# A delta-rule attention between two FFNs: kept sign of the state, q e^G on GpSimd, softplus summed from PSUM, LZ's first values in one call, and a new order of the pass

## The chip, the cores and the metric

The kernel runs on one core of a Trainium2 chip. The metric is the device time of one execution in microseconds; lower is better. The engines are TensorE (PE; its weight loads are PEld), VectorE (DVE), ScalarE (ACT), GpSimd (POOL) and SyncE (SP), each with its own instruction stream. They meet only at semaphores.

## What is computed

The input x is 8 sequences of 256 tokens with 256 channels. The output is x plus half an FFN, then plus an attention, then plus half an FFN again; all is float32. The FFN phases are not touched. The attention has 16 heads with key and value size 128 and four keys and values (R = 4) per token. Projections pass a causal convolution of four taps and SiLU. Then, for chunks (cut from the reference):

```python
kexp = kg * jnp.exp(Gg)[:, :, :, None, :]
rhs = (vg - jnp.einsum('bhtid,bhdv->bhtiv', kexp, S)).reshape(b, h, C * Rr, dv)
u = jax.scipy.linalg.solve_triangular(M, rhs, lower=True, unit_diagonal=True)
qhat = qg * jnp.exp(Gg)
o = SCALE * (jnp.einsum('bhtd,bhdv->bhtv', qhat, S) + o_intra)
S_new = jnp.exp(glast)[..., None] * S + jnp.einsum('bhtid,bhtiv->bhdv', kdec, u)
```

G is the running sum of log_alpha = -exp(A_log) * softplus(g_raw + dt_bias). At the end o is normalised, gated and projected by Wo.

## The kernel before

Three phases follow each other: FFN, attention, FFN. In the attention the tokens are cut into 4 blocks of 512 (NT), each of two sequences, and each block is worked through head by head: 64 units s = 16 n + h. Chunks are of 8 tokens in 4 groups (32 tokens, 128 rows of keys), so a unit has 16 chunks u = 8 hb + c: two sequences (hb = 0, 1), of 8 steps (c = 0 to 7) each, which the state S ties together.

One loop over p (a **pass**) is written out in each engine's function, as a list of calls in an order found beforehand and fixed by hand; nothing is decided at run time. In a pass, four units are at work at different stages: projection, convolution and decay for p, products and factors for p - 1, inverse for p - 2, the last steps and the output for p - 3. The lists of all engines start with steps 3 to 7 of unit p - 3, and end with steps 0 to 2 of unit p - 2.

The names that matter:
- project_k(b) (b = 4 is q), project_v(b), decay, gate: TensorE products of 512 columns into bank 0 or 1 of PSUM. bank_use lays out in turn which of the two a product takes and which semaphore frees it. tap_k/tap_v (ScalarE) copies the bank times the last tap into acc, conv_k/conv_v (VectorE) add three more taps out of the bank, silu_k/silu_v (ScalarE) write KQ and V.
- decay on ScalarE (Abs, Exp, Ln), above (Relu) and softplus on VectorE give sp_t; add_up sums it into C; distance(l) takes differences of C into rn, factors(l) are their exponentials Fl, Fe and F0; levels(q, l) on VectorE gives X = KQ times Fl for quarter q.
- products(q, l) on TensorE multiplies X with itself into banks 2 and 3. evacuate(q, l) on VectorE copies bank 2 masked into Pd, keep(q) on ScalarE bank 3 into E and At. products(q + 1, 0) waits for both.
- take, norm, weigh (VectorE) build LA from Pd. begin and rows (GpSimd) clear LZ, set its first values and eliminate row by row; unfold and turn (VectorE) bring the result into Zc and Ztc; place, first to fourth (TensorE and ScalarE) make the inverse Ztf of it.
- spread(q, what) on GpSimd is kdec (what 0) and kexp (1): KQ times e^(G end - G) or e^G (Fe). turn on TensorE transposes kdec. query (VectorE) makes qn, the product of q and -e^G.
- One step: rhs (TensorE, kexp times S; VectorE makes Rs), solve (TensorE; ScalarE copies to Us), update (TensorE: kdT times Us, At times Us, S times qn; VectorE makes the new S). In between stands S with alternating sign from step to step, by the SUB at its end; qn's sign and rhs's ADD fit that.
- out_square (ScalarE) squares the output, mean_square (TensorE) sums it, out_root and gated normalise, output multiplies by WO.

The same engine serves all four units in turn, so a late operand holds up everything behind it on that engine. ScalarE needs another function table for SiLU and Tanh than for Exp and Ln; preload_act_table_set and the compiler place the loads (ACT_TABLE_LOAD).

Of the kernel before, what the change touches and what calls it, by code (L numbers as in the profile page):

```python
# [88 lines left out]
def build(nc, x, out, wkq, wv, wo, vec, wf1, wg1, wb, bg1, wu, wd, fvec, wsd, cst, B, H):  # L89
# [4 lines left out]
    with ctx:  # L94
# [22 lines left out]
        half_c = [cs[:, C_SEL + 16 + half:C_SEL + 17 + half] for half in range(2)]  # L117
# [453 lines left out]
        LZ = sb("LZ", [P, 32, 16])  # L571
# [31 lines left out]
        v_max, v_kq, v_d, v_qn, v_X, v_Pd, v_bd = (sem(f"v_{n}") for n in ("max", "kq", "d", "qn", "X", "Pd", "bd"))  # L603
# [4 lines left out]
        g_zero, g_kdec, g_kexp, g_copy, g_X0, g_init, g_row = (sem(f"g_{n}") for n in ("zero", "kdec", "kexp", "copy", "X0", "init", "row"))  # L608
# [3 lines left out]
        def turns(order, count):  # L612
# [117 lines left out]
        def delta_tensor(e):  # L730
# [176 lines left out]
            def update(s, hb, c):  # L907
# [13 lines left out]
                if c:  # L921
                    ins = mm(o, S[:, hb, c % 2, :], qn[:, s % 2, 32 * u:32 * u + 32], False, True)
# [1012 lines left out]
```

## Time and profile before

| | |
|---|---|
| median of 3 runs | 5054.45 us |
| lowest to highest | 5050.53 to 5068.83 us |
| the profiled execution | 5059.32 us |
| its span, first to last instruction | 5057.5 us |
| TensorE, VectorE, ScalarE, GpSimd busy | 90, 82, 69, 64% of the span |
| mean granted clock of TensorE | 0.967 |

The profile is one execution, taken with the hardware profiler. Busy time is the union of an engine's instructions; idle time is put down to the semaphore event that ended it. The span's first 330 us are the first FFN and the ramp of the attention, its last 260 us the second FFN; between them passes of the loop repeat. The granted clock is the share of TensorE's full 2.4 GHz that was let through.

### The profile page before, as it was taken

The numbers are of one execution on the slowest core, as the hardware profiler recorded it, in microseconds if no ns is written. First come the engines' busy times: TensorE is split into PE (matmuls) and PEld (weight loads), VectorE is DVE, ScalarE is ACT, GpSimd is POOL, SyncE is SP. The second block draws the span as 40 slices with busy tenths as digits, with TensorE's granted clock in tenths as the row PEclk, the third lists the DMA queues.
The fourth block names the chain that finished last, engine by engine and source line by source line (L and its number), as shares of the span: only waits on it lengthen the run. The fifth ranks groups of instructions, "written<-read, shape, count | busy, mean of one in ns | idle before, by whom it ended". The sixth has DMA issues, their size and how long they took to land.

```text
span 5057.5 us, 151421 instructions
## 1 busy us (share of the span) xinstructions
PE 4558.3 (90%) x63200; PEld 3167.2 (63%) x63200; DVE 4143.8 (82%) x7262; ACT 3476.3 (69%) x6771; POOL 3221.5 (64%) x5316
## 2 busy tenths in 40 slices
PE   8869999999999999999999999899999999998889
PEld 5436666666666666666666666666666666666655
DVE  3278998888888889889999889988899888998422
ACT  3267777777777777777777777777777777777421
POOL 0047777776677766777767777667777777767500
PEclk9989999999999999999999999999999999999769
DMA  2110000000100000000100000000000000000010
GB/s 89 65 48 20 25 25 25 25 13 25 33 31 21 21 25 25 25 14 24 33 31 29 24 14 25 25 25 20 22 29 25 25 25 14 25 25 9 3 45 18
DMA packets 49724, 135.45 MB, mean 27 GB/s; under 512 B 7056, under 2 KB 28176, under 8 KB 48400
## 3 DMA queue, kind: packets, MB, share of 16 engines
q1 hardware_dynamic: 49040, 125.77, 7.2%
q8 instruction: 498, 8.16, 0.7%
q14 instruction: 186, 1.52, 0.1%
HBM read 111.60 MB, written 14.16 MB: 25 GB/s over the span
## 4 chain that ended last, share of the span: by engine, by line
PE 55%; DVE 26%; ACT 11%; issue 6%; POOL 1%; DMA 1%; SPq 0%; DVEq 0%; ACTq 0%
PE bank L734 46%; DVE acc L1392 8%; PE bank L256 7%; DVE X L1389 7%; DVE sp_t L1389 2%; ACT L1299 2%; DVE Pd L1497 2%; ACT Us L1048 1%; ACT o L1049 1%; DVE Zc L1576 1%; DVE o L1392 1%; DVE Rs L1392 1%; PE bank L805 1%; ACT L1329 1%; DVE x1m L1389 1%
## 5 line engine op out<-in xcount | busy, mean ns | idle before, releaser
L1392 DVE SCALAR_TENSOR_TENSOR acc<-bank,vc,acc 128x510 f32<-128x510 f32 (+2 forms) x1728 | 1271.4, 739 | 144.6 <-ACT acc L1048 118.9
L1813 POOL TENSOR_TENSOR LZ<-LZ,LT 128x120 f32<-128x120 f32 (+26 forms) x1984 | 961.6, 485 | 155.5
L1810 POOL TENSOR_TENSOR LT<-LA,LZ 128x120 f32<-128x120 f32 (+26 forms) x1984 | 913.4, 460 | 145.8
L1389 DVE TENSOR_TENSOR X<-KQ,Fl 128x640 f32<-128x640 f32 x1024 | 1004.3, 997 | 1.5 <-ACT Fl L1049 1.5
L1783 POOL COPY X<-KQ 128x640 f32<-128x640 f32 x256 | 246.8, 964 | 928.6 <-PE bank L734 311.8
L734 PE MATMUL bank<-X 128*32 128x60 f32 (+1 forms) x32768 | 656.2, 206 | 134.6 <-DVE Pd L1497 87.2
L734 PEld LDWEIGHTS bank<-X 128*32 128x32 f32 x32768 | 529.3, 112 | 370.3 <-issue 210.7
L1048 ACT ACTIVATE Us<-bank 128x128 f32<-128x128 f32 x1024 | 280.8, 276 | 628.5 <-PE bank L734 622.5
L734 PE MATMUL bank<-xnTm,WK 128*128 128x512 f32 x1280 | 663.3, 644 | 47.2 <-DVE acc L1392 33.8
L734 PE MATMUL bank<-Rs,Ztf 128*128 128x128 f32 x2048 | 475.6, 319 | 67.9 <-DVE Rs L1392 47.5
L1762 POOL TENSOR_TENSOR kdec<-KQ,Fe 128x512 f32<-128x512 f32 x256 | 339.0, 1324 | 297.9 <-PE bank L805 297.9
L1392 DVE SCALAR_TENSOR_TENSOR Rs<-V,knT,bank 128x128 f32<-128x128 f32 x896 | 308.4, 344 | 257.9 <-PE bank L734 246.3
L734 PE MATMUL bank<-xnTm,WV 128*128 128x512 f32 x1024 | 498.4, 609 | 12.8 <-ACT sg L1049 7.4
L734 PE MATMUL bank<-Us,kdT 128*128 128x128 f32 x1792 | 412.3, 313 | 71.5 <-ACT Us L1048 56.7
L734 PEld LDWEIGHTS bank<-Rs,Ztf 128*128 128x128 f32 x2048 | 322.0, 194 | 195.6 <-DVE Rs L1392 116.1
L1048 ACT ACTIVATE acc<-bank,vc 128x512 f32<-128x512 f32 x576 | 394.0, 684 | 66.7 <-PE bank L734 63.3
L734 PEld LDWEIGHTS bank<-xnTm,WK 128*128 128x128 f32 x1280 | 232.1, 201 | 284.0 <-issue 190.3
L734 PE MATMUL bank<-S,kexp 128*128 128x128 f32 x1792 | 393.3, 302 | 5.0 <-ACT S L1048 3.4
L1762 POOL TENSOR_TENSOR kexp<-KQ,Fe 128x512 f32<-128x512 f32 x256 | 388.6, 1528 | 0.0
L734 PEld LDWEIGHTS bank<-Us,kdT 128*128 128x128 f32 x1792 | 275.6, 194 | 137.6 <-ACT Us L1048 125.8
L734 PE MATMUL bank<-qn,S 128*128 128x32 f32 x1792 | 353.9, 280 | 0.0
L734 PEld LDWEIGHTS bank<-S,kexp 128*128 128x128 f32 x1792 | 286.7, 195 | 79.0 <-issue 32.8
(145 smaller groups left out, 9370.0 us busy)
## 6 DMA issues: line engine op xcount, KB each, us to landing
WK<-in_wkq SPq DMA_DIRECT2D x64, 704.0 KB, 6.1
WV<-in_wv SPq DMA_DIRECT2D x64, 576.0 KB, 3.9
WO<-in_wo SPq DMA_DIRECT2D x64, 128.0 KB, 2.0
wuh<-in_wu SPq DMA_DIRECT2D x2, 1024.0 KB, 7.6
xt<-in_x SPq DMA_DIRECT2D x4, 512.0 KB, 6.5
wuh_d<-wuh SPq DMA_DIRECT2D x1, 2048.0 KB, 6.3
x_d<-x SPq DMA_DIRECT2D x4, 512.0 KB, 3.1
xnT_d<-xT SPq DMA_DIRECT2D x4, 512.0 KB, 2.7
```

Source lines behind the costliest of these rows:

```text
L256: return e.matmul(o, l, r, start=start, stop=stop, skip_group_check=True)
L734: return e.matmul(o, l, r, start=start, stop=stop, skip_group_check=True)
L805: ins = e.transpose(o[:, P * c:P * c + P], kdec[:, c, :], ident)
L1048: return e.activation(o, i, f, scale=scale)
L1299: e.preload_act_table_set("natural_log_exp_and_others")
L1389: return e.tensor_tensor(o, a, b, op)
L1392: return e.scalar_tensor_tensor(out=o, in0=a, scalar=sc, in1=b, op0=op0, op1=op1)
L1497: return e.copy_predicated(o, mk, d.rearrange("p n (a c) -> p n a c", c=c))
L1762: return e.tensor_tensor(o.rearrange("p u (g i t) -> p (u g) i t", g=4, i=R), kq[:, 16 * q:16 * q + 16, 0:R, :], f.unsqueeze(2).broadcast_ ...
L1783: e.tensor_copy(X0[:, :, 0:40], kk.rearrange("p g i t -> p g (i t)")).then_inc(g_copy, 1)
L1810: e.tensor_tensor(tmp, LA[:, j + 1:32, 8 * (j % R) + j // R].unsqueeze(2).broadcast_to([P, rr, cc]), LZ[:, j, 0:cc].unsqueeze(1).broadcast ...
L1813: e.tensor_tensor(LZ[:, j + 1:32, 0:cc], LZ[:, j + 1:32, 0:cc], tmp, SUB).then_inc(g_row, 1)
```

## The change

- *The state keeps its sign.* S is written by adding, Rs by subtracting, and the copy at step 0 has no factor -1.
- *q e^G on GpSimd.* query leaves VectorE's list and stands in GpSimd's as one tensor_tensor, with semaphore g_qn instead of v_qn. The wait for it moves from a unit's first update to the matmul that reads qn.
- *Softplus.* above writes the Relu back into the PSUM bank, softplus adds the bank and rn.
- *LZ's first values.* After the memset one tensor_tensor over 8 x 2 x 2 elements, in place of four tensor_scalar over 8; LZ's tile gets 16 elements longer for the view.
- *Order.* The lists of calls of all four engines and the turns of the two banks and three acc are laid out anew. One preload before factors(3) and one before decay(2) are gone.

```diff
-        half_c = [cs[:, C_SEL + 16 + half:C_SEL + 17 + half] for half in range(2)]
+        half_c = cs[:, C_SEL + 16:C_SEL + 18]
...
-        LZ = sb("LZ", [P, 32, 16])
+        LZt = sb("LZ", [P, 8 * 66])
+        LZ = LZt[:, 0:512].rearrange("p (r c) -> p r c", c=16)
+        LZd = LZt[:, :].rearrange("p (t x) -> p t x", x=66)[:, :, 0:64].rearrange("p t (h y) -> p t h y", y=32)[:, :, :, 0:18:17]
...
-            ("decay", 0, 0, a_relu, 1, 0), ("v", 1, 1, v_cv, 12, 5), ("k", 3, 0, v_ck, 15, 11),
+            ("decay", 0, 0, v_sp, 1, 0), ("k", 3, 0, v_ck, 15, 11), ("ms", 0, 3, a_ms, 3, 0),
...
-                    w.wait_ge(v_qn, every(s, 1))
...
                 if c:
+                    w.wait_ge(g_qn, every(s, 1))
                     ins = mm(o, S[:, hb, c % 2, :], qn[:, s % 2, 32 * u:32 * u + 32], False, True)
...
-                act(sp_t[:, :], bank[bank_use["decay", 0, s][0]][:, :], ACT.Relu, bias=dtb[:, h:h + 1]).then_inc(a_relu, 1)
+                raw = bank[bank_use["decay", 0, s][0]][:, :]
+                act(raw, raw, ACT.Relu, bias=dtb[:, h:h + 1]).then_inc(a_relu, 1)
...
-                act(S[:, hb, 1, :], bank[5 + hb][:, 2 * P:3 * P], ACT.Copy, scale=-1.0).then_inc(a_S, 1)
+                act(S[:, hb, 1, :], bank[5 + hb][:, 2 * P:3 * P], ACT.Copy).then_inc(a_S, 1)
...
-                tt(sp_t[:, :], sp_t[:, :], rn[:, 0, :], ADD).then_inc(v_sp, 1)
+                w.wait_ge(a_F, every(s - 1, 12))
+                tt(sp_t[:, :], bank[bank_use["decay", 0, s][0]][:, :], rn[:, 0, :], ADD).then_inc(v_sp, 1)
...
-                stt(Rs[:, hb, :], V[:, s % 2, u, :], knT[:, s % 2, u:u + 1], bank[5 + hb][:, 0:P], MUL, ADD).then_inc(v_Rs, 1)
+                stt(Rs[:, hb, :], V[:, s % 2, u, :], knT[:, s % 2, u:u + 1], bank[5 + hb][:, 0:P], MUL, SUB).then_inc(v_Rs, 1)
...
-                    MUL, SUB).then_inc(v_S, 1)
+                    MUL, ADD).then_inc(v_S, 1)
...
+                w.wait_ge(p_o, every(s - 2, 16))
+                e.tensor_tensor(qn[:, s % 2, :].rearrange("p (g t) -> p g t", t=8), KQ[:, s % 2, :, R, :],
+                                Fe[:, 0, :].rearrange("p (g t) -> p g t", t=8), MUL).then_inc(g_qn, 1)
...
-                        e.tensor_scalar(flat[:, a:a + 463:66], Cn[:, :, 2 * hf + k], half_c[hf], None,
-                                        MUL).then_inc(g_init, 1)
+                e.tensor_tensor(LZd, Cn[:, :, :].rearrange("p t (h k) -> p t h k", h=2),
+                                half_c.unsqueeze(1).unsqueeze(3).broadcast_to([P, 8, 2, 2]), MUL).then_inc(g_init, 1)
```

**TensorE from mean_square to output.** Rows of the program before, then of the changed one (o,cs is mean_square, WK a projection of k or q, X products, WO output, fgm,WV the gate):

```order
L734 MATMUL bank<-o,cs 128x512
L734 MATMUL bank<-xnTm,WK 128x512 x2
L734 MATMUL bank<-X 32x60 x16
L734 MATMUL bank<-X 32x20 x32
L734 MATMUL bank<-X 32x40 x8
L734 MATMUL bank<-X 32x80 x8
L734 MATMUL bank<-WO,o 128x256 x4
L734 MATMUL bank<-fgm,WV 128x512
L796 MATMUL bank<-cs,V 128x128 x4
```

```order
L736 MATMUL bank<-o,cs 128x512
L736 MATMUL bank<-X 32x60 x16
L736 MATMUL bank<-X 32x20 x16
L736 MATMUL bank<-xnTm,WK 128x512 x2
L736 MATMUL bank<-X 32x20 x16
L736 MATMUL bank<-X 32x40 x8
L736 MATMUL bank<-X 32x80 x8
L736 MATMUL bank<-fgm,WV 128x512
L736 MATMUL bank<-WO,o 128x256 x4
L736 MATMUL bank<-xnTm,WV 128x512 x4
```

project_k(4) stood directly behind mean_square and now has products(1,0) and (1,1) ahead of it; the gate went from behind the output to ahead of it; turn_v(0) left this place.

**ScalarE from the last of steps 0 to 2 into the next pass.** Us is the copy of solve, Fl a factor, KQ silu_k, acc a tap, kdT the transposed kdec; before, then now:

```order
L1048 ACTIVATE Us<-bank 128x128 x2
L1299 ACT_TABLE_LOAD
L1049 ACTIVATE Fl<-rn,posA 128x32x8
L1049 ACTIVATE Fl<-rn,negA 128x32x8
L1048 ACTIVATE Us<-bank 128x128
L1048 ACTIVATE kdT<-bank 128x512
L1049 ACT_TABLE_LOAD
L1049 ACTIVATE KQ<-acc 128x64x8 x2
L1048 ACTIVATE acc<-bank,vc 128x512
L1048 ACTIVATE Us<-bank 128x128
L1048 ACTIVATE kdT<-bank 128x512
```

```order
L1051 ACTIVATE Fl<-rn,posA 128x16x16
L1051 ACTIVATE Fl<-rn,negA 128x16x16
L1050 ACTIVATE Us<-bank 128x128 x3
L1051 ACT_TABLE_LOAD
L1051 ACTIVATE KQ<-acc 128x64x8
L1050 ACTIVATE Us<-bank 128x128
L1050 ACTIVATE kdT<-bank 128x512
L1051 ACTIVATE KQ<-acc 128x64x8
L1050 ACTIVATE acc<-bank,vc 128x512
L1050 ACTIVATE Us<-bank 128x128
L1051 ACTIVATE KQ<-acc 128x64x8
L1308 ACT_TABLE_LOAD
```

A load stood between two Us, with factors(3) behind it; now the factors come ahead of the last steps' Us and the three silu_k stand under one load.

**VectorE, the softplus sum and the evacuations of the first two quarters.** sp_t is the sum, X levels, Pd evacuate, knT lengths, acc a convolution, o gated; before (the sum then stood much later in the pass) and now:

```order
L1392 SCALAR_TENSOR_TENSOR acc<-bank,vc,acc 128x2x254
L1392 SCALAR_TENSOR_TENSOR acc<-bank,vc,acc 128x2x253
L1392 SCALAR_TENSOR_TENSOR acc<-bank,vc,acc 128x2x255
L1392 SCALAR_TENSOR_TENSOR acc<-bank,vc,acc 128x2x254
L1497 COPY_PREDICATED Pd<-cs,bank 128x80
L1392 SCALAR_TENSOR_TENSOR acc<-bank,vc,acc 128x2x253
L1497 COPY_PREDICATED Pd<-cs,bank 128x40x2
L1497 COPY_PREDICATED Pd<-cs,bank 128x20x4
L1392 SCALAR_TENSOR_TENSOR qn<-KQ,Fe 128x512
L1392 SCALAR_TENSOR_TENSOR o<-sg,o 128x512
L1392 SCALAR_TENSOR_TENSOR o<-bank,hon,o 128x512
```

```order
L1392 SCALAR_TENSOR_TENSOR Rs<-V,knT,bank 128x128
L1558 STREAM_TRANSPOSE knT<-kn 128x32
L1392 SCALAR_TENSOR_TENSOR Rs<-V,knT,bank 128x128
L1389 TENSOR_TENSOR sp_t<-bank,rn 128x512
L1389 TENSOR_TENSOR X<-KQ,Fl 128x640
L1489 COPY_PREDICATED Pd<-cs,bank 128x80
L1389 TENSOR_TENSOR X<-KQ,Fl 128x640
L1489 COPY_PREDICATED Pd<-cs,bank 128x40x2
L1392 SCALAR_TENSOR_TENSOR acc<-bank,vc,acc 128x2x255
L1489 COPY_PREDICATED Pd<-cs,bank 128x20x4
L1392 SCALAR_TENSOR_TENSOR acc<-bank,vc,acc 128x2x254
L1392 SCALAR_TENSOR_TENSOR acc<-bank,vc,acc 128x2x253
```

The two evacuations that stood behind four convolutions now stand between X and convolutions, qn is gone, and sp_t and knT have come in behind the last two Rs.

## Rows read from the trace of the kernel before

**Rows 1.** The page: busy us of each engine, its share of the span, instructions.

```profile
PE 4558.3 (90%) x63200; PEld 3167.2 (63%) x63200; DVE 4143.8 (82%) x7262; ACT 3476.3 (69%) x6771; POOL 3221.5 (64%) x5316
```

**Rows 2.** LZ's memset; a stretch: its us, each engine's busy us, clock, DMA, GB/s.

```profile
L1792 POOL MEMSET LZ<- x64: 521/525/527, 332.4 to 4745.0; 128x512 f32 x64
...
1400.00:2400.00 1000.00, 915.21 (x13692) 644.05 (x13692) 891.74 (x1552) 741.01 (x1461) 719.79 (x1188) 0.98 0.07 24
```

**Rows 3.** TensorE's waits between 400 and 4600 us: us in total, times, longest.

```profile
PE bank L734 <- DVE Pd L1497: 78.8, 55, 1.5
PE bank L734 <- ACT Us L1048: 54.2, 120, 0.5
PE bank L734 <- ACT o L1049: 46.7, 60, 0.8
PE bank L734 <- issue: 42.4, 78, 2.1
PE bank L734 <- DVE Rs L1392: 39.4, 120, 0.4
PE bank L734 <- DVE acc L1392: 26.2, 60, 0.4
```

**Rows 4.** The chain that ended last, 2500 to 2572 us: start, us, what.

```profile
2533.23 1.28 ACT L1049
...
2540.16 0.57 DVE acc L1392
...
2549.53 1.09 DVE Zc L1576 x2
...
2560.90 1.67 DVE sp_t L1389
2562.79 1.52 issue
```

**Rows 5.** TensorE's timeline: start, us, what, idle time before it and its releaser.

```profile
2502.77 1.96 PE L734 MATMUL bank<-xnTm,WK 128*128 128x512 f32 x4
...
2539.25 1.10 PE L734 MATMUL bank<-o,cs 128*128 128x512 f32 x2 [0.78 <-ACT o L1049]
2540.78 3.56 PE L734 MATMUL bank<-xnTm,WK 128*128 128x512 f32 x4 [0.43 <-DVE acc L1392]
...
2564.59 0.63 PE L734 MATMUL bank<-X 128*32 128x60 f32 x32 [1.44 <-DVE Pd L1497]
```

**Rows 6.** Stretches of 2 us behind mean_square, in two passes; columns as in Rows 2.

```profile
2540.96:2542.96 2.00, 2.00 (x3) 0.79 (x4) 1.34 (x4) 1.90 (x5) 1.76 (x4) 0.52 0.00 0
2542.96:2544.96 2.00, 2.00 (x57) 0.69 (x57) 0.95 (x2) 0.58 (x1) 1.61 (x6) 0.63 0.00 0
...
2682.96:2684.96 2.00, 1.71 (x100) 1.07 (x99) 1.59 (x3) 1.44 (x4) 1.75 (x4) 1.00 0.00 0
```

**Rows 7.** Timelines of VectorE and GpSimd in the later half of a pass.

```profile
2560.81 1.76 DVE L1389 TENSOR_TENSOR sp_t<-sp_t,rn 128x512 f32<-128x512 f32 x1
...
2565.18 0.78 DVE L1389 TENSOR_TENSOR X<-KQ,Fl 128x640 f32<-128x640 f32 x1
...
2566.89 1.27 POOL L1762 TENSOR_TENSOR kdec<-KQ,Fe 128x512 f32<-128x512 f32 x1 [3.19 <-PE bank L805]
```

**Rows 8.** Groups of instructions: count, busy us, mean ns; then one row of GpSimd's timeline.

```profile
L1389 DVE TENSOR_TENSOR x1m<-bank,x1m 128x512 f32<-128x512 f32 x128 | 88.6, 692 | 15.5 <-PE bank L734 15.4
...
L1392 DVE SCALAR_TENSOR_TENSOR qn<-KQ,Fe 128x512 f32<-128x512 f32 x64 | 43.8, 684 | 0.0
...
L1798 POOL TENSOR_SCALAR LZ<-Cn,cs 128x8 f32<-128x8 f32 x256 | 123.7, 505 | 6.4
...
2545.51 0.22 POOL L1810 TENSOR_TENSOR LT<-LA,LZ 128x16 f32<-128x16 f32 x1
```

**Rows 9.** ScalarE's timeline around the load ahead of factors(3).

```profile
2513.93 1.28 ACT L1299 ACT_TABLE_LOAD   x1
...
2516.04 0.26 ACT L1048 ACTIVATE Us<-bank 128x128 f32<-128x128 f32 x1
```

More of the change, by code:

```diff
@@ L606, in build @@
         v_Rs, v_S, v_o, v_out = (sem(f"v_{n}") for n in ("Rs", "S", "o", "out"))
-        g_zero, g_kdec, g_kexp, g_copy, g_X0, g_init, g_row = (sem(f"g_{n}") for n in ("zero", "kdec", "kexp", "copy", "X0", "init", "row"))
+        g_zero, g_kdec, g_kexp, g_qn, g_copy, g_X0, g_init, g_row = (sem(f"g_{n}") for n in ("zero", "kdec", "kexp", "qn", "copy", "X0", "init", "row"))
         def turns(order, count):
@@ L964, in delta_tensor @@
                 solve(p - 3, 0, 5)
-                products(p - 1, 0, 3)
                 rhs(p - 3, 1, 5)
@@ L968, in delta_tensor @@
                 solve(p - 3, 1, 5)
+                products(p - 1, 0, 2)
+                rhs(p - 3, 0, 6)
+                products(p - 1, 0, 3)
+                update(p - 3, 1, 5)
                 decay(p)
-                rhs(p - 3, 0, 6)
-                update(p - 3, 1, 5)
+                rhs(p - 3, 1, 6)
+                solve(p - 3, 0, 6)
                 products(p - 1, 0, 4)
-                solve(p - 3, 0, 6)
-                rhs(p - 3, 1, 6)
                 solve(p - 3, 1, 6)
@@ L1030, in delta_tensor @@
                 update(p - 2, 1, 0)
+                project_k(p + 1, 2)
+                rhs(p - 2, 1, 1)
                 update(p - 2, 0, 1)
-                rhs(p - 2, 1, 1)
-                turn(p - 1, 2)
+                solve(p - 2, 1, 1)
                 rhs(p - 2, 0, 2)
-                solve(p - 2, 1, 1)
                 update(p - 2, 1, 1)
                 solve(p - 2, 0, 2)
+                products(p, 0, 0)
                 rhs(p - 2, 1, 2)
                 update(p - 2, 0, 2)
-                products(p, 0, 0)
                 solve(p - 2, 1, 2)
+                rhs(p - 2, 0, 3)
+                update(p - 2, 1, 2)
         def delta_scalar(e):
@@ L1677, in delta_vector @@
                 rhs(p - 3, 0, 7)
[L1678 to L1689 removed]
+                lengths(p - 2)
+                rhs(p - 3, 1, 7)
+                softplus(p)
+                levels(p - 1, 1, 2)
+                evacuate(p - 1, 0, 1)
+                levels(p - 1, 1, 3)
+                evacuate(p - 1, 0, 2)
+                conv_k(p, 3, 2)
+                evacuate(p - 1, 0, 3)
+                conv_k(p, 3, 1)
+                conv_k(p, 3, 0)
+                levels(p - 1, 1, 4)
                 gated(p - 3, 0)
+                levels(p - 1, 2, 1)
                 gated(p - 3, 1)
@@ L1713, in delta_vector @@
                 conv_v(p - 1, 3, 0)
+                levels(p - 1, 3, 1)
+                levels(p - 1, 3, 2)
                 evacuate(p - 1, 2, 0)
                 evacuate(p - 1, 2, 1)
-                evacuate(p - 1, 2, 2)
-                levels(p - 1, 3, 1)
-                softplus(p)
-                levels(p - 1, 3, 2)
-                evacuate(p - 1, 2, 3)
-                clamp(p)
-                lengths(p - 2)
                 levels(p - 1, 3, 3)
                 add_up(p)
+                clamp(p)
                 levels(p - 1, 3, 4)
+                evacuate(p - 1, 2, 2)
                 distance(p, 1)
+                evacuate(p - 1, 2, 3)
+                conv_k(p + 1, 0, 2)
+                conv_k(p + 1, 0, 1)
                 evacuate(p - 1, 3, 0)
+                conv_k(p + 1, 0, 0)
                 evacuate(p - 1, 3, 1)
+                scale(p)
                 evacuate(p - 1, 3, 2)
```

275 lines of the change are left out of this document (124 added, 151 removed).

## The prediction, made before the changed kernel ran

> **What bounds the kernel now.** I read the page first, then where time is evenly spent, then the waits, then the chain. The page [rows 1] has TensorE busy 90% of the span, VectorE 82%, ScalarE 69%, GpSimd 64%. The middle phase is nearly all of it: GpSimd clears LZ once per head and block, 64 times between 332.4 and 4745.0 us [rows 2], so a pass of the loop takes (4745.0 - 332.4) / 63 = 70.0 us. A stretch of 1000 us [rows 2] says that in it TensorE is busy 91.5%, VectorE 89% and GpSimd 72%, at a mean granted clock of 0.98; the one behind it reads the same within 1%. TensorE idles about 6 us of each pass. That, and what the clock loses, is all that can be won: no matrix product is removed. The waits of TensorE between 400 and 4600 us, which are 60 passes [rows 3], divide it, per pass: 78.8 / 60 = 1.31 us for Pd (products(3,0) needs the last evacuate of quarter 2), 54.2 / 60 = 0.90 for Us, 46.7 / 60 = 0.78 for the squared output ahead of mean_square, 42.4 / 60 = 0.71 for issue, 39.4 / 60 = 0.66 for Rs, 26.2 / 60 = 0.44 for acc (project_k(4), whose bank is still read by the convolution).
>
> The chain of one pass [rows 4] shows why Pd is late. From 2549.5 to 2562.6 it runs on VectorE alone: the unfolding into Zc, four X, six acc, X and the softplus sum sp_t. VectorE is thus the limit of the later half of a pass, although its busy share is the lower one. Earlier in the pass the chain goes over a table load on ScalarE and three convolutions to project_k(4), 0.43 us late [rows 4, 5]. From there I call the start of mean_square, 2539.25 [rows 5], M.
>
> **The clock.** The four matmuls of project_k(4) take 3.56 us in this pass, those of another projection 1.98 [rows 5]. The granted clock is 0.52 in the 2 us from 2540.96, that is the 1.2 GHz level, and 1.00 at the same place two passes later [rows 6]; of ten passes looked at, three fell. TensorE had idled 0.78 and 0.43 us ahead of the fall. By the mean of 0.98 the clock costs 0.02 x 70 = 1.4 us a pass. One fall costs (1 - 0.52) x 2 + (1 - 0.63) x 2 = 1.7 us [rows 6].
>
> **The change, part by part.** *The sign of the state* changes the scale of a copy and the second operator of three VectorE forms, and no count or shape: 0.
>
> *The softplus sum.* It took 1.76 us as sum of two SBUF tensors while GpSimd ran kdec and kexp; an equal sum with one operand in PSUM (x1m) has a mean of 0.69 [rows 7, 8]. VectorE gets 1.76 - 0.69 = 1.07 us back. The Relu now writes into the bank, so that the bank is freed by the sum instead of by the Relu: its next user is mean_square. Laying the rows end to end, the sum ends some 3 us ahead of M. Cost 0; if decay were 3 us late, every further us would stand ahead of mean_square.
>
> *The product q e^G* leaves VectorE, 0.68 us [rows 8], and costs GpSimd about what kdec costs there, 1.27 us [rows 7]. GpSimd is idle 28% of the time [rows 2], 19.6 us a pass, so there it is free. It is put between kdec of quarter 2 and kexp of quarter 3. Its first reader on TensorE comes most of a pass later. What it does delay, by its own 1.3 us, is kexp of quarter 3, for which the next head's Fe on ScalarE waits: the rows put that kexp's end at M + 29.7 and Fe at M + 31.4. 0 on the path, and 1.3 if that cover were gone.
>
> *LZ's first values.* Four calls of 0.505 us [rows 8] become one with 32 elements. No row has that form; a product of 16 elements takes 0.22 [rows 8], and four of the old calls 2.0: between these I take 0.4, as it is one instruction on few elements. GpSimd's elimination, from the clearing of LZ to the unfolding, gets 1.6 us shorter, and another 1.3 since kdec of quarter 3 no longer stands in it. The unfolding, which now stands earlier on VectorE (about M + 7 rather than M + 10), then still finds it finished, by about 1 us.
>
> *Table loads.* ScalarE had seven per pass and has four, by the order of both; each takes 1.28 us, so 3.85 us of its time go. Off the bound, but one of them stood between two Us [rows 9]: the Us copy at 2516.04 came late, and update(0,3) waited for it 0.54 us.
>
> *The new order* decides the rest. I added the durations of the rows from M on, each engine in its new order.
> - Us. update(0,1) now has project_k(2) ahead of it, and update(0,3) has no table load ahead of its Us: both waits (0.90) go. But update(1,0) comes 0.3 us behind solve(0,1), and update(0,5) directly behind rhs(1,5); I put 0.4 for these. Net -0.5.
> - project_k(4) has the first two products of quarter 1 ahead of it, 1.0 us of TensorE work, and the convolutions of k3 end in that time: -0.44.
> - The bank of output(0) was mean_square's and is now project_k(4)'s. It is free when the convolutions of k4 are done. ScalarE copies k4 only behind both roots, a table load and silu_v(0): M + 4.3 to 5.0. Three convolutions of 0.74 end at M + 7.3. TensorE is there at M + 6.3: a new wait of **+1.0**. Bounds 0.2 (as the edge of this kind now costs) and 2.0 (VectorE late by one more operation).
> - Pd. VectorE has the softplus sum and one X fewer ahead of the unfolding's successors, but three X, the running sum, clamp and distance(1) are pulled ahead of the last evacuate of quarter 2; TensorE has project_k(0) and half of the second inverse pulled ahead of products(3,0). The rows put the evacuate's end at M + 26.3 and TensorE at M + 26.4: the wait of 1.31 shrinks to 0.1, **-1.2**. The bounds are -1.31 and +0.5, since the adding-up has no collisions beyond two.
> - Rs and S between steps 3 and 7: a pass now has 2 us less other work between its steps. I put **+0.2**; bounds 0 and 1.0.
> - mean_square still stands right behind the last update: 0.78 stays. Issue stays.
> - Clock. The 0.43 us behind the 0.78 goes, but 1.0 us of idling comes 6 us later. I take **-0.4** of 1.4; bounds -1.4 and +0.7.
>
> Sum per pass: -0.5 - 0.44 + 1.0 - 1.2 + 0.2 - 0.4 = -1.34 us. The prologue, the epilogue and both FFN phases are untouched. Over 63 passes -84 us. The profiled execution took 5059.3 us with a span of 5057.5, the median of the runs is 5054.45; 5059.3 - 84 = 4975, and against the median **4970 us**.
>
> **Two rules of the skill.** The collision of VectorE and GpSimd is in the rows: an X takes 0.78 us alone, and the sum of two SBUF tensors takes 1.76 while GpSimd multiplies [rows 7]. The Trainium skill (GPSIMD Engine Reference, Specifications) states that GpSimd's SBUF interfaces are shared with VectorE, with contention for VectorE instructions with two SBUF inputs. It speaks against moving q e^G: a ninth product per pass is on the shared interface. By it the moved product can take up to its own 1.27 us back from VectorE instead of giving 0.68.
> The sum out of PSUM is measured at 0.69 us [rows 8]. The Trainium skill (VectorE: DVE Perf Modes, the section on the TRN2 errata) gives PSUM sources a larger fixed part than SBUF sources, 120 cycles to 58, by which, as an estimate, 0.06 us of the gain would be lost; the trace's row is used.
>
> **Rivals.** *A: more collisions.* Slower. Four operations of VectorE are doubled in a pass now, about 1.0 us each (two X, sp_t, rn). In the new order GpSimd's kexp of quarters 1 and 2 and kdec of quarter 1 come at about M + 16 to M + 21, over levels(3,1) to levels(3,3); kdec of quarter 2, q e^G and kexp of quarter 3 over scale and distance(1), kdec of quarter 3 over distance(2). If six are hit instead of four, VectorE gets 2.0 us more, in the half of the pass where it is the limit, and TensorE pays all of it: -1.34 + 2.0 = +0.66, 5054 + 42 = 5096. It decides as soon as the collisions outgrow the slack, which after the sum above is about zero. For it: nine products instead of eight and a nearly full VectorE. Against: the unavoidable waits of GpSimd for kdec's bank spread them, and softplus is out of it.
> The skill's rule above is this rival's mechanism; the trace agrees on the collisions of today and cannot show the new ones.
> *B: the clock.* The idle of 1.0 us ahead of output(0) joins the 0.78 and the clock falls in every pass: 1.7 a pass and other losses of 0.4, so 2.1 instead of 1.4. The sum is -1.34 + 0.4 + 0.7 = -0.24, 5039. For it: three of ten passes fall behind 1.2 us of idling spread over 2.5. Against: here 3.8 us of dense work lie between.
> *C: VectorE is clear of the path.* Convolutions of k4 end as TensorE arrives (-0.8), and the clock hardly falls (-0.8 more): -2.9 a pass, 4870. For it: 1.75 us of VectorE work and 3.85 of ScalarE's are gone for certain.
> *D: nothing arrives.* The order trades waits one for one; it gives about B's time and is counted there.
>
> **Chances.** Forecast 0.52 (4920 to 5020), A 0.16, B and D 0.18, C 0.14. About 0.5%, 25 us, is what a measurement of this kernel can tell from no change. Faster by more: 0.52 + 0.14 + 0.02 of B = 0.68; within: 0.16; slower: 0.16. The range reaches into C and A, 4890 to 5075, and leaves about 0.2 out.
>
> **What would show it.** The clearings of LZ should come 68.7 us apart. TensorE's waits: Us below 30 us, Pd below 20 in 60 passes, acc at output(0) up to 60, o unchanged near 47. VectorE: sp_t at 0.69 a piece, about 1.7 us less busy per pass. ScalarE: 4 x 64 table loads, not 7 x 64. GpSimd: qn near 1.3 us. Wrong would be: X and rn with a larger mean (A); a mean clock at or below 0.97 (B); the unfolding waiting for LZ, or more than 2 us of waits for Rs, then steps 3 to 7 have become a latency chain, for which I allowed 0.2.

## The result, and the profile after

The changed kernel takes **5279.07 us** (median of 4 runs, 5271.58 to 5306.96), against 5052.49 us for the kernel before on the same chip. The ratio is **1.0461**, with a 95% interval of 1.0431 to 1.0491. The forecast was 4970 us in a range up to 5075: wrong in sign, and 204 us above the upper end.

The page of the changed kernel, as [rows 1]: busy us of each engine; below it the DMA queues (packets, MB, share of 16 engines).

```profile
PE 4729.6 (90%) x63200; PEld 3382.8 (64%) x63200; DVE 3918.7 (74%) x7198; ACT 3197.8 (61%) x6572; POOL 3048.7 (58%) x5188
...
q1 hardware_dynamic: 49040, 125.77, 6.8%
q8 instruction: 498, 8.16, 0.6%
```

LZ's memset and the stretch of [rows 2], of the changed kernel:

```profile
L1792 POOL MEMSET LZ<- x64: 524/524/528, 337.6 to 4990.6; 128x512 f32 x64
...
1400.00:2400.00 1000.00, 905.46 (x13194) 657.85 (x13192) 798.38 (x1449) 651.12 (x1355) 636.34 (x1075) 0.92 0.07 24
```

A pass takes (4990.6 - 337.6) / 63 = 73.86 us against 70.04 [rows 2]: +3.8. VectorE, ScalarE and GpSimd all have less to do. TensorE is as busy as before, but at a granted clock of 0.92 instead of 0.98, so that it gets less done: 13194 matmuls in the stretch, against 13692.

Its waits between 400 and 4600 us, as [rows 3], here 57 passes:

```profile
PE bank L736 <- issue: 150.6, 63, 4.4
PE bank L736 <- DVE acc L1392: 108.7, 114, 1.9
PE bank L736 <- DVE Rs L1392: 46.5, 166, 0.5
PE bank L736 <- ACT o L1051: 44.4, 57, 0.8
PE bank L736 <- ACT Ztf L1050: 13.2, 56, 0.2
```

The waits for Pd and Us are gone. Those for semaphores went about as planned. The first row did not: **issue**, idle time that no semaphore ends, was 42.4 us over 60 passes [rows 3] and is 150.6 over 57. From here on I call a piece of it, over 0.15 us long, a **stand**.

One such stand, on TensorE's timeline (start, us, what, idle time before it), in a pass whose mean_square starts at 2581.82 (M):

```profile
2581.82 1.10 PE L736 MATMUL bank<-o,cs 128*128 128x512 f32 x2 [0.78 <-ACT o L1051]
...
2589.58 1.75 PE L736 MATMUL bank<-WO,o 128*128 128x256 f32 x7 [1.64 <-DVE acc L1392]
...
2591.47 3.71 PE L736 MATMUL bank<-xnTm,WV 128*128 128x512 f32 x8
2595.41 0.69 PE L736 MATMUL bank<-Zc,E 32*32 32x32 f32 x32 [0.24 <-ACT Ztf L1050]
2596.03 1.50 PE L736 MATMUL bank<-X 128*32 128x60 f32 x112
...
2597.52 0.19 PE L736 MATMUL bank<-Ys,Ztf 32*32 32x32 f32 x1
2600.31 0.22 PE L736 MATMUL bank<-Ztf,Ys 32*32 32x32 f32 x2 [2.60 <-issue]
```

TensorE stops in the middle of second(0), between two matmuls that have no wait between them in the program. Ahead of the stop run project_v(3), first(0) and products(2,0) to products(2,3) without a break. From first(0) to products(2,4) there are 208 short matmuls, each with its weight load: 416 instructions. (The trace has every float32 matmul as two.) I call them **the run**. Stretches of 2 us of the same pass (columns as in Rows 2: us, busy us of PE, PEld, DVE, ACT, POOL, clock, DMA share, GB/s):

```profile
2594.00:2596.00 2.00, 1.76 (x35) 0.77 (x33) 2.00 (x4) 1.31 (x2) 0.00 (x0) 1.00 0.00 0
2596.00:2598.00 2.00, 1.71 (x123) 1.51 (x115) 1.97 (x4) 1.07 (x2) 1.24 (x2) 1.00 0.89 279
2598.00:2600.00 2.00, 0.00 (x0) 0.00 (x0) 1.93 (x4) 0.00 (x0) 2.00 (x3) 1.00 1.05 230
2600.00:2602.00 2.00, 1.69 (x61) 1.63 (x61) 2.00 (x2) 0.83 (x3) 0.64 (x1) 0.69 0.94 385
2602.00:2604.00 2.00, 2.00 (x17) 1.45 (x13) 1.68 (x5) 0.91 (x3) 0.00 (x0) 0.50 0.42 172
...
2614.00:2616.00 2.00, 2.00 (x6) 0.80 (x6) 2.00 (x4) 1.11 (x3) 0.00 (x0) 0.90 0.00 0
```

Three things coincide: 123 matmuls in 2 us, the DMA engines full from 2596 to 2602 (SyncE's load_wv and load_wk, 576 and 704 KB, issued when project_v(3) is done), and TensorE at a stand. Behind it the clock goes to 0.50, the 1.2 GHz level, until 2614.4. Over passes 3 to 59, a 128x512 matmul takes 1103 ns at that level and 611 at the full clock, one of 128x128 429 and 298, and the shortest 237 and 192.

What is late is the program itself. The queue q8 moved 498 packets of 8.16 MB / 498 = 16.4 KB. TensorE's records are 127,591 (63,200 matmuls, as many weight loads, 1,191 of its sequencer), 256 to a packet: q8 carries TensorE's instructions, some 7.5 packets a pass. The DMA queues from M + 3.2 to M + 15.8, and in the 1.6 us behind that:

```profile
q1 hardware_dynamic: 232, 0.54, 14.6%
...
q1 hardware_dynamic: 180, 0.44, 116.8%
q8 instruction: 1, 0.02, 4.2%
```

In the first stretch there is no packet of q8, and the next one comes when q1 already fills the engines. That packet takes from 2597.74 to 2598.81; TensorE had stopped at 2597.71 and goes on at 2600.31, 1.5 us after the landing.

The records settle that this is no coincidence. I numbered TensorE's records in the order of their start. Modulo 256, all 69 stands of passes 3 to 59 of the changed kernel come at the number 193 or 194, and all 453 stands of 1 us or more in the 14 kernels below at 193 to 195. Behind each of these 453, TensorE goes on 1.2 to 1.65 us after the packet for the next block has landed. Such a stand is thus a wait for the next packet, in the kernel before too. (Some 40 of the stands there, of 0.3 us at M + 4, come at any number and are of another kind.)

The Trainium skill (Runtime: NRT & Kernel Launch, Instruction fetch mechanics) has instructions fetched in blocks of 256 while earlier ones run, at a cost "mostly hidden". The blocks agree with the 498 packets and with the places of the stands; the cost is not hidden here, 2.88 us a pass.

**All passes.** I counted passes 3 to 59 of every kernel (a pass is from one mean_square to the next; a fall is a spell of the 1.2 GHz level; the last four columns are us per pass).

| kernel | ratio to before | us a pass | stands | other waits | us at 1.2 GHz |
|---|---|---|---|---|---|
| before | 1 | 70.14 | 0.70 | 4.65 | 2.2 |
| after | 1.0461 | 74.25 | 2.88 | 3.78 | 12.3 |
| e1_late_loads | 0.9834 | 68.56 | 1.28 | 3.78 | 2.9 |
| e2_before_late_loads | 1.0001 | 70.12 | 0.63 | 4.73 | 2.2 |
| e3_late_wk | 1.0204 | 72.17 | 2.12 | 3.76 | 9.2 |
| e4_edits_old_order | 0.9992 | 70.22 | 0.75 | 4.64 | 2.5 |
| e5_late_spread | 0.9867 | 68.95 | 1.03 | 3.83 | 3.7 |
| e6_spread | 1.0318 | 72.65 | 2.63 | 3.86 | 8.7 |
| e7_double_loads | 1.0516 | 74.44 | 3.24 | 3.76 | 11.9 |
| e8_before_loads_on_run | 1.0182 | 71.55 | 1.37 | 4.70 | 3.7 |
| e9_after_loads_on_second_run | 1.0112 | 71.13 | 2.19 | 3.70 | 6.8 |
| e10_late_v_inside | 0.9835 | 69.16 | 0.45 | 5.47 | 2.2 |
| e11_late_products_ahead | 0.9602 | 67.17 | 0.45 | 4.15 | 0.4 |
| e12_products_ahead | 0.9626 | 67.21 | 0.49 | 4.15 | 0.2 |

Passes with neither fall nor stands over 0.3 us take 68.80 us before (14 of 57) and **65.79** after (7 of 57). The plan itself was good, by 3.0 us a pass. Seven passes are few, but the undisturbed passes of e1 (13) and e7 (4) take 65.86 and 65.83. The mean of all passes of the changed kernel is 8.5 us above 65.79: 2.9 are the stands, and the other 5.6, which I put down to the 12.3 us at half clock, are the remainder.

### The profile page after: what moved, and what is told of

Read it like the earlier page. It is cut to its first block, busy times and chain, and to the rows that moved or that the text cites. A ratio compares the mean times of both kernels' runs of the same rounds, so it can differ in the third digit from the quotient of the medians.

```text
span 5281.2 us, 150966 instructions
## 1 busy us (share of the span) xinstructions
PE 4729.6 (90%) x63200; PEld 3382.8 (64%) x63200; DVE 3918.7 (74%) x7198; ACT 3197.8 (61%) x6572; POOL 3048.7 (58%) x5188
## 3 DMA queue, kind: packets, MB, share of 16 engines
q8 instruction: 498, 8.16, 0.6%
## 4 chain that ended last, share of the span: by engine, by line
PE 65%; DVE 15%; ACT 10%; issue 9%; POOL 1%; DMA 0%; DVEq 0%; SPq 0%; ACTq 0%; POOLq 0%
PE bank L736 52%; PE bank L256 7%; DVE acc L1392 4%; PE bank L798 4%; ACT Ztf L1050 2%; PE bank L807 2%; DVE LA L1523 2%; ACT acc L1050 2%; ACT o L1051 2%; ACT L1051 2%; DVE Zc L1568 1%; DVE Rs L1392 1%; DVE X L1389 1%; DVE rn L1389 1%; DVE Ztc L1576 1%
## 5 line engine op out<-in xcount | busy, mean ns | idle before, releaser
L1809 POOL TENSOR_TENSOR LZ<-LZ,LT 128x120 f32<-128x120 f32 (+26 forms) x1984 | 931.4, 469 | 155.5
L1389 DVE TENSOR_TENSOR X<-KQ,Fl 128x640 f32<-128x640 f32 x1024 | 944.6, 932 | 0.0
L736 PE MATMUL bank<-xnTm,WK 128*128 128x512 f32 x1280 | 695.9, 671 | 24.9 <-DMA WK<-in_wkq 12.2
L736 PE MATMUL bank<-X 128*32 128x60 f32 (+1 forms) x32768 | 614.3, 206 | 77.0 <-issue 66.5
L1783 POOL COPY X<-KQ 128x640 f32<-128x640 f32 x256 | 184.9, 722 | 645.3 <-PE bank L736 348.3
L736 PEld LDWEIGHTS bank<-xnTm,WK 128*128 128x128 f32 x1280 | 253.7, 214 | 276.2 <-issue 252.0
L736 PE MATMUL bank<-Us,kdT 128*128 128x128 f32 x1792 | 387.7, 299 | 20.5 <-ACT Us L1050 0.2
L736 PE MATMUL bank<-S,kexp 128*128 128x128 f32 x1792 | 376.3, 298 | 0.6 <-ACT S L1050 0.2
L1439 DVE TENSOR_SCALAR rn<-bank 128x512 f32<-128x512 f32 x64 | 44.2, 691 | 411.3 <-PE bank L736 411.3
L736 PEld LDWEIGHTS bank<-Zc,E 32*32 32x32 f32 (+1 forms) x6144 | 256.3, 137 | 144.2 <-ACT Ztf L1050 89.4
```

Of the source, the lines that this page charges most:

```text
L736: return e.matmul(o, l, r, start=start, stop=stop, skip_group_check=True)
L1389: return e.tensor_tensor(o, a, b, op)
L1783: e.tensor_copy(X0[:, :, 0:40], kk.rearrange("p g i t -> p g (i t)")).then_inc(g_copy, 1)
L1809: e.tensor_tensor(LZ[:, j + 1:32, 0:cc], LZ[:, j + 1:32, 0:cc], tmp, SUB).then_inc(g_row, 1)
```

## The experiments

The theories by letter: **S**, bulk loads that fall on a run of short matmuls keep TensorE's instruction packets waiting. **R**, the run asks for instructions faster than they can come, loads or none. **W**, the longer wait at output(0) lowers the clock, and that is the root. Where an edit is "late loads", it is this line ahead of SyncE's loads of a pass:

```
+                if 0 <= p - 2 < NS:
+                    w.wait_ge(p_rhs, nth(p - 2, 14, 1))
                 s = p - 1
                 if 0 <= s < NS:
...
                         load_wv(s + 2)
```

It holds them until rhs(1,1). In e1 they move mostly from M + 39 to M + 45, where TensorE starts some 20 to 30 matmuls in 2 us, against 141 in the densest 2 us of the run. Nothing else differs.

### Loads late, in the changed kernel, in the kernel before, and in part; and the edits without the order

*e1_late_loads*: the changed kernel with late loads.

> The changed kernel; SyncE issues the loads of WV and WK (and of the block's inputs) only when rhs(1,1) of unit p - 2 is done, some 38 us behind mean_square instead of 14. Nothing else changes. Theory S (supply): in the changed kernel TensorE stands 2 to 4 us inside the second inverse or products of quarter 2, where it waits for no semaphore, because its next instructions are fetched by DMA behind 1.28 MB of weight loads; that idle time then drops the clock. Expected: the stalls under 'issue' fall from 150 us to under 50, mean granted clock of the middle phase 0.98 or more, passes 66 to 67 us apart, 4800 to 4860 us. Rival R (run): the run of short matmuls outpaces the fetch, whatever the loads do: stalls stay, 5230 to 5290 us. Rival W (wait): the clock falls because of the 1.64 us wait for acc ahead of the output: it stays too, clock near 0.92, over 5200 us.

Measured: 4978.96 us, ratio **0.9834** [0.9797, 0.987]. One line takes 300 us away, and the kernel beats both. But it misses what was expected by 120 us. Its waits:

```profile
PE bank L738 <- DVE acc L1394: 116.5, 122, 1.9
PE bank L738 <- issue: 75.4, 62, 1.9
```

The wait for acc at output(0) is as long as in the changed kernel (1.64 us a piece), while the passes with a fall are down from 42 to 14: W is out. Stands of 1.1 to 1.9 us are left inside the run in 31 of 57 passes, with no load in sight. So S holds for most of it, and R for a part.

*e2_before_late_loads*: the kernel before with the same line.

> The kernel before, with the same delay of the loads. Theory S: it too loses something to the fetch, but has less short work in one run; its waits under 'issue' are 42 us in 60 passes and its clock 0.98. At most these go: 5057 - 40 - 50 = 4960, at least 5040. Rivals R and W: no change, 5045 to 5060.

Measured: 5055.04 us, ratio 1.0001 [0.9985, 1.0016]. That is in the range of R and W; S had expected 5040 at most. In the old order the loads cost nothing that can be measured: stands are 0.63 us a pass instead of 0.70.

*e3_late_wk*: the line stands only ahead of load_wk, 704 of 1280 KB.

> The changed kernel, with the load of WK alone delayed (0.70 of the 1.28 MB); WV stays where it is. Theory S: the burst ends some 2 us behind its start instead of 4, so the fetch is late by 2 us less: about half or more of the loss goes, 4850 to 5080 us. Rivals R and W: 5230 to 5290 us.

Measured: 5163.51 us, ratio 1.0204 [1.0168, 1.024], outside what was expected: 116 us of the 300 that late loads win, where half or more had been expected. 576 KB in the same place are enough for stands of 2 us and more in 30 of 57 passes.

*e4_edits_old_order*: the order of before, with the sign, q e^G on GpSimd, and LZ's values in one call; the softplus sum stays in SBUF, and the preloads stay.

> The kernel before, its order of calls kept, with the sign of the state, q e^G on GpSimd (between kexp of quarter 2 and kexp of quarter 3) and LZ's first values in one call; the softplus sum stays in SBUF. My theory of the parts: VectorE gets 0.68 us a pass back ahead of gated, where it waits for ScalarE, GpSimd 1.6 us: 0 to -0.5 us a pass, 5020 to 5055 us. A rival in which one of these edits is itself the cost of the change (more collisions on GpSimd) expects over 5080.

Measured: 5049.73 us, ratio 0.9992 [0.9967, 1.0016]. That is within what was expected. These edits alone are worth nothing that can be measured. What the change gives and takes is in the order, with the softplus sum and the two preloads that go with it.

### Run spread out, loads doubled

*e5_late_spread* and *e6_spread* change TensorE's list at one place; e5 has the late loads as well.

```
                 products(p - 1, 2, 1)
+                second(p - 2, 0)
                 products(p - 1, 2, 2)
+                turn_v(p - 2, 0)
                 products(p - 1, 2, 3)
-                second(p - 2, 0)
-                products(p - 1, 2, 4)
-                turn_v(p - 2, 0)
                 third(p - 2, 0)
                 turn_v(p - 2, 1)
+                products(p - 1, 2, 4)
```

> The changed kernel with the late loads of the first run, and TensorE's order of one stretch spread: second(0) stands after products(2,1), turn_v(0) after products(2,2), third(0) after products(2,3), and products(2,4) last, so that longer matmuls of the turns and third lie between the groups of short ones. Theory R (the run first(0), products(2,0..3), second(0), products(2,4) asks for instructions faster than they arrive, whatever the loads do): the idle time of TensorE that nothing ends by a semaphore falls from 1.28 us a pass (late loads alone) to under 0.6, and falls of the clock with it; period 67.2 to 68.0 against 68.56, so 4895 to 4945 us. Rival (the rest of the stalls is another cause, or second(0) now waits for GpSimd's or VectorE's part of first): stalls stay at 1.2 us or semaphore waits at second(0) appear, 4970 to 5030 us.

Measured: 4984.77 us, ratio 0.9867 [0.9842, 0.9892]. Stands 1.03 instead of 1.28 us, 22 passes with a fall instead of 14: a miss, in the rival's range. In first(0), products(2,0), products(2,1), second(0) and products(2,2) there are still 176 matmuls together, with their weight loads 352 instructions, more than a packet has.

> The changed kernel with TensorE's order spread in the same way, and the loads where the change has them. Theory S (SyncE's bulk loads hold back the instruction packets of TensorE's queue): the packet is late by as much as before, but it is wanted later or earlier only by the phase of the pass, so stalls fall from 2.9 us a pass to 1.5 to 2.5 and the time from 5279 to 5100 to 5220 us. Theory R (the density of the run alone): stalls under 1 us a pass and 4900 to 5000 us. If neither bears: 5250 to 5300 us.

Measured: 5208.94 us, ratio 1.0318 [1.0284, 1.0351]. The time is within the range of S. Its 1.5 to 2.5 us of stands were 2.63.

*e7_double_loads*: SyncE copies about as many bytes from memory to memory once more, ahead of load_wv.

```
+                        w.wait_ge(p_gate, every(s, 1))
+                        w.wait_ge(p_v, every(s, 4))
+                        w.wait_ge(d_spare, 32 * s)
...
+                        e.dma_start(spare_d[0, :, 0:nk], ws).then_inc(d_spare, 16)
+                        e.dma_start(spare_d[1, :, 0:nv], vs).then_inc(d_spare, 16)
                         load_wv(s + 2)
```

> The changed kernel with copies from memory to memory of about the bytes of one pass's WK and WV issued just ahead of the loads, at the same place of the pass; no engine waits for them but SyncE. Theory S: the instruction packet lies behind twice the burst, stalls grow from 2.9 us a pass to 4.5 to 7, the half clock with them, and the time is 5380 to 5650 us. Theory R: stalls as in the changed kernel, 5270 to 5320 us.

Measured: 5311.95 us, ratio 1.0516 [1.0479, 1.0554]. The time is in the range of R, not of S: stands 3.24 us, not 4.5 to 7, and the interval overlaps that of the changed kernel. The loads now move from M + 14 to M + 22 instead of M + 14 to M + 18. The mere form of S, that a packet waits until the burst is over, falls: twice the bytes cost 0.36 us more of stands. R alone falls by e1, whose run is the same. I therefore took each packet's delay from the records: a packet begins when TensorE has come to a certain instruction, so the time since it passed the earliest such place among the neighbouring packets says how late it is. Of the packets due at M + 14 to M + 16, the mean is 1.8 us with late loads (72 packets), 4.0 in the changed kernel (73), 4.7 with the doubled ones (72). (With more or fewer neighbours each mean moves by up to 0.4.) So a burst costs a packet some 2 to 3 us, whether it is long or very long. The delay is an inference from start times; no row shows the request for a packet.

### Loads moved onto another run

Both hold the loads until total(p), so that they move at M + 23 to M + 28 in e8 and mostly at M + 25 to M + 29 in e9, onto the second run of short matmuls.

```
+                if 0 <= p < NS:
+                    w.wait_ge(p_norm, every(p, 1))
                 s = p - 1
```

*e8_before_loads_on_run*, in the kernel before:

> The kernel before, with SyncE holding the loads of WV and WK until total(p), so that they move some M+23 to M+28, on the kernel's own second run of short matmuls (products(3,0), first(1), products(3,1), second(1), products(3,2), products(3,3)). Theory S (bulk loads that fall on a run of short matmuls hold back TensorE's instructions, in any order of the work): idle time of TensorE that nothing ends grows from 0.7 to 1.5 to 2.5 us a pass, part of the passes lose the clock, 5110 to 5280 us. Rival (the loads only hurt the changed order, by something else in it): no change, 5045 to 5065 us.

Measured: 5145.67 us, ratio 1.0182 [1.0142, 1.0222]. That is within the range of S. So the old order can be hurt in the same way; S does not hang on the new one. TensorE's waits:

```profile
PE bank L736 <- DVE Pd L1499: 83.1, 58, 1.5
PE bank L736 <- issue: 82.7, 84, 3.2
```

The wait for Pd stays, issue doubles against [rows 3]. Stands of 1.5 us and more appear behind M + 26 in 24 of 57 passes; in the kernel before there was none. The stands come to 1.37 us a pass, a little under what was expected.

*e9_after_loads_on_second_run*, in the changed kernel:

> The changed kernel with the same hold, until total(p): the loads leave the first run (M+14) and meet the second (second(1), products(3,0) to products(3,4), M+26 to M+28). Theory S: the stalls move with the loads, from M+16 to M+28, 2 to 3 us a pass, falls follow them there, 5120 to 5280 us. Rival (only the place of the first run is at fault, and any later time for the loads is as good as the latest): 4970 to 5000 us as with the loads at M+38.

Measured: 5114.11 us, ratio 1.0112 [1.0075, 1.0148], 6 us under the range. Stands of 2 us and more went from M + 16 to M + 28, in 20 passes; all 20 fell there. The place of the loads decides where the stands are.

### The run cut by a long product

*e10_late_v_inside*: late loads, and project_v(3) between products(2,1) and products(2,2); second(0) also moves, ahead of products(2,3).

> The changed kernel with the loads at M+38, and project_v(3), two long matmuls' pairs of some 1.9 us with few instructions, put between products(2,1) and products(2,2) instead of ahead of the run. Theory R (what stalls are left come from the run's density alone, with packets that take their usual time): stalls at M+14 to M+20 go from 0.8 to under 0.2 us a pass, and with them most falls of the clock (14 of 57 passes with late loads alone); 66.8 to 67.6 us a pass, 4870 to 4920 us. Rival: as with late loads alone, 4970 to 4990 us.

Measured: 4981.62 us, ratio 0.9835 [0.9808, 0.9863]. All stands at M + 14 to M + 24 are gone, 0 of 57 passes, as R says. The time did not follow and lies in the rival's range, for project_v(3) had been the cover of another wait:

```profile
PE bank L738 <- ACT Ztf L1052: 119.0, 61, 2.0
...
PE bank L738 <- issue: 26.2, 27, 1.9
```

first(0) now waits 1.96 us for Ztf in every pass, and the clock falls behind that in 19 of 57, without a stand.

*e11_late_products_ahead* and *e12_products_ahead* put two products ahead of project_v(3) instead, e11 with late loads, e12 with the loads where the change has them.

```
+                products(p - 1, 2, 0)
+                products(p - 1, 2, 1)
                 project_v(p - 1, 3)
                 first(p - 2, 0)
-                products(p - 1, 2, 0)
-                products(p - 1, 2, 1)
                 products(p - 1, 2, 2)
-                products(p - 1, 2, 3)
                 second(p - 2, 0)
+                products(p - 1, 2, 3)
                 products(p - 1, 2, 4)
```

> The changed kernel with the loads at M+38, and TensorE's order changed in one place: products(2,0), products(2,1), project_v(3), first(0), products(2,2), second(0), products(2,3), products(2,4). The 64 short matmuls and loads of products(2,0..1) run ahead of project_v(3), whose 1.9 us cover the wait for Ztf that cost 1.96 us with project_v(3) inside the run. Theory: no stall at M+14 to M+20 as in that run, first(0) waits at most 0.3 us, so a pass takes 66.0 plus 0.4 of stalls at M+28 plus some 0.6 for the clock that is left, 67.0, 4870 to 4910 us. Rival (the clock falls for other reasons in a third of the passes whatever the stalls are, as 19 of 57 did there): 68.0 to 68.6 a pass, 4930 to 4980 us.

Measured: **4854.87 us**, ratio **0.9602** [0.9573, 0.9631], below the range by 15 us. Its interval and that of e12, below, overlap.

> The changed kernel with the same change of TensorE's order, and the loads where the change has them, M+14 to M+18. If bulk loads alone make the stalls: as the changed kernel, 5250 to 5290 us. If the run's density alone: as with the loads late, 4870 to 4980 us. If it takes both, dense run and loads at once: stalls under 1 us a pass, some passes still fall, 4920 to 5060 us.

Measured: 4869.68 us, ratio 0.9626 [0.9601, 0.965]. Taken by itself this is the lower edge of "the run's density alone" in the expectation, and below the range of "both". The four kernels together say more:

| | loads where the change has them | loads late |
|---|---|---|
| the change's order | 5279.07 (after) | 4978.96 (e1) |
| two products ahead of project_v(3) | 4869.68 (e12) | 4854.87 (e11) |

Loads cost 300 us on the long run and 15 on the shortened one, where the intervals overlap; the long run costs 124 us without loads and 409 with them. With 64 short matmuls (128 instructions with their weight loads) fewer behind project_v(3), 144 instead of 208, the loads may stay where they were. The large loss takes both, a dense run and loads at once; some 30% of it comes with the run alone. The waits and the same place of a pass in e12 (stretches from M + 13.4 on):

```profile
PE bank L736 <- DVE acc L1392: 116.4, 122, 1.9
PE bank L736 <- DVE Rs L1392: 52.3, 186, 0.5
PE bank L736 <- ACT o L1051: 49.0, 63, 0.8
PE bank L736 <- DVE Pd L1489: 41.6, 63, 3.0
PE bank L736 <- issue: 28.4, 31, 1.9
```

```profile
2190.00:2192.00 2.00, 2.00 (x28) 0.76 (x28) 1.97 (x4) 0.15 (x1) 2.00 (x3) 1.00 0.00 0
2192.00:2194.00 2.00, 1.90 (x125) 1.71 (x121) 0.96 (x2) 1.49 (x4) 2.00 (x2) 1.00 0.54 118
2194.00:2196.00 2.00, 2.00 (x33) 1.69 (x28) 1.93 (x4) 1.62 (x4) 0.10 (x1) 1.00 1.01 417
```

The DMA engines are as full as in the changed kernel (1.01, 417 GB/s), the matmuls as dense (125 in 2 us), but the density is over when the burst comes. At this place TensorE has no stand over 0.6 us in 57 passes, and the clock stays at 1.00. The new wait for Pd, 0.66 us a pass, is the price of the earlier products.

**Do the stands bring the falls?** For the run at M + 14 (and the one at M + 28 in e8 and e9), by the longest stand in it:

| kernel | stand of 2 us or more: passes, with a fall | shorter or none: passes, with a fall |
|---|---|---|
| after | 42, 42 | 15, 0 |
| e1 | 0, 0 | 57, 11 |
| e3 | 30, 28 | 27, 5 |
| e5 | 1, 1 | 56, 16 |
| e6 | 35, 34 | 22, 6 |
| e7 | 45, 44 | 12, 2 |
| e8 | 15, 15 | 42, 17 |
| e9 | 20, 20 | 37, 2 |
| e10 | 0, 0 | 57, 19 |
| e12 | 0, 0 | 57, 0 |

Of the 17 falls of e8 without a long stand, ten come at M + 26, behind the wait for Pd, as ten do in the kernel before; the 19 of e10 come behind the wait of 1.96 us for Ztf. The 11 of e1 all follow a stand of 1.1 to 1.9 us. Over all kernels, behind M + 13, a fall began during or within 5.5 us behind 3 of 223 stands below 1 us, 41 of 145 from 1 to 1.5, 59 of 104 from 1.5 to 2, and 184 of 188 above. In the same place with the same loads the clock falls when TensorE stood long, and does not when it didn't. That bulk loads lower the clock by themselves is excluded by e12.

## Why the prediction was wrong

**The step that failed is "Issue stays".** The stands rose from 0.7 to 2.9 us a pass, and brought most of 5.6 more through the clock. The rows had the warning: 42.4 us of issue, the longest 2.1 [rows 3], and 1.52 us of it in the chain [rows 4]. I took idle time that no semaphore ends for a constant of the kernel. It is the wait for TensorE's next packet of instructions, and depends on how many short matmuls follow each other and on what the DMA engines do then; the change altered the first, and I didn't lay the loads beside the list. Neither load had moved: both come behind project_v(3), as before. TensorE's run had: it puts 123 matmuls into the 2 us in which the loads begin, where the order before had two products ahead of project_v(3), as e12 has again.

**Clock, -0.4 with bounds -1.4 and +0.7.** Measured, the share at 1.2 GHz went from 2.2 to 12.3 us a pass, at 5.6 us for 12.3 that is +4.6: far outside the bounds. I had bounded it by a fall behind each of the two short waits, 1.7 us, the shortest falls of the rows; behind the stands of 2 us and more in the changed kernel they last 10 to 17 us. The bounds missed on the other side too. I had looked at ten passes only in 12 us each, around mean_square; of passes 3 to 59 of the kernel before, ten fell at M + 26, behind the wait for Pd, for 6.8 us each, and the change takes that wait away. Rival B, "the clock falls in every pass", named the right effect (42 of 57 passes), with the wrong cause and little more than a third of the price (2.1 a pass).

The other steps, per pass, read from the waits above:
- Us -0.5, Rs +0.2: Us went wholly (-0.90), Rs is 46.5 / 57 = 0.82, +0.16. Net -0.74, against -0.3.
- project_k(4) -0.44: went. But another projection waits 0.26 for acc at M + 45, which I had not seen.
- output(0) +1.0: **+1.64**, in every pass, within the bounds.
- Pd -1.2: -1.31, gone.
- mean_square 0.78 stays: it did.
- The semaphore waits together went from 4.65 to 3.78, -0.87; the forecast without the clock was -0.94. That the sums agree is partly luck: output(0) is 0.64 above its term and the wait of 0.26 was not in it, while Us with Rs is 0.44 below.
- What I did not forecast: an undisturbed pass is 3.0 us shorter. In passes without a fall TensorE's busy time is 1.5 us shorter (63.3 to 61.8) with the same matmuls, whose durations add up to nearly the same (230.6 to 230.2 us), so that they overlap more. In e12, with hardly a stand left in the run, it is 62.0: most of this gain does not need the long run. Why they overlap more is not shown. It also means that the forecast would have been off without the stands: e12 takes 4870 us, 100 below it and below the range.

Rival A, more collisions, went the other way. Groups of VectorE, before and after:

```profile
L1389 DVE TENSOR_TENSOR X<-KQ,Fl 128x640 f32<-128x640 f32 x1024 | 1004.3, 997 | 1.5 <-ACT Fl L1049 1.5
```

```profile
L1389 DVE TENSOR_TENSOR X<-KQ,Fl 128x640 f32<-128x640 f32 x1024 | 944.6, 932 | 0.0
L1389 DVE TENSOR_TENSOR sp_t<-bank,rn 128x512 f32<-128x512 f32 x64 | 43.7, 683 | 4.6 <-ACT rn L1051 4.6
```

An X takes 932 ns instead of 997. The rule of the Trainium skill that was this rival's mechanism (GPSIMD Engine Reference, Specifications) took nothing back here that can be seen. e4 is the cleaner test, as it has the moved product in the old order: an X takes 1003 ns against 997 there, while q e^G itself takes 1860 on GpSimd. The sum sp_t takes 683 ns as forecast (0.69). qn takes 1316 ns on GpSimd (forecast 1.3). LZ's first values take 1.17 us, not 0.4: the one call with 32 elements in a view of three steps costs more than twice one of the old calls of 8 (0.505), and my bound of 0.22, from 16 elements in a row, was no bound. It is off the path. Four table loads a pass, as forecast.

Rival C, 4870 us with VectorE clear of the path, is the time of e12, 4870, though VectorE's convolutions still hold output(0) for 1.64 us there: the number agrees by luck, the gain came from elsewhere.

## What to carry to other kernels

TensorE's own program comes as DMA traffic, 16 KB for every 256 instructions, and competes with the kernel's loads. When an order is laid out, put on one time axis the count of TensorE instructions per 2 us and the bulk loads: here TensorE stood up to 4.4 us in a run of 208 short matmuls beside the loads and up to 1.9 us without them, and 0.6 us at most in one of 144. Keep bulk loads off such a run, and cut it with a long product, if that covers no wait where it stood. A stand of this kind can be told from others in the records: it comes at the same number modulo 256, to within two, each time. Idle time called issue in the middle of a block without waits is a price that an order can multiply; read where it stands, and what follows it in the clock.

## What the runs showed of the hardware

- TensorE's instructions come by queue q8, 498 packets for 127,591 records, 256 each. TensorE stops at a block's end when the next packet is late, and goes on 1.2 to 1.65 us after its landing (453 stands of 1 us or more). Where a packet is due in a dense run, it begins 1.8 us late with quiet DMA queues and 4.0 us late during 1.28 MB of loads, by my count of the records; doubling the bytes made it 4.7. How the packet is served among the other queues is open.
- A stand of TensorE of 2 us or more was followed by the 1.2 GHz level in 183 of 187 passes of six kernels, for 7 to 17 us at a time, but in e8 for 3.4 us, once 6.8. Of the stands from 1.5 to 2 us somewhat over half did (59 of 104), of those from 1 to 1.5 over a quarter (41 of 145). The semaphore wait of 1.96 us in e10 did so in 19 of 57 passes. What separates passes with the same wait is open.
- Stands of up to 1.9 us in the second run, at M + 28, are left in e11 and e12 (0.4 us a pass), and the 1.64 us at output(0). Nothing was tried against either.
